# Decoder layer on one core: the weighed values of cross attention turned and divided by VectorE in 32x32 blocks, in place of transposes on TensorE and bank copies

## What is computed

```
q, k, v = x @ Wq, x @ Wk, x @ Wv             # q and k are then rotated
w   = softmax(q k^T / 4 + mask)              # over the tokens of x
a_w = tanh(gate) * softmax(q a_k^T / 4)      # over the adapter, a_k = ctx @ Wk
attn = w @ v + a_w @ a_v                     # per head
x = layernorm(x + attn @ Wo)
```

## Time and profile before

| | us |
|---|---|
| median of three runs | 2985.49 (2984.8 to 2992.0) |
| the profiled execution | 2984.0 |
| its span, first to last instruction | 2982.2 |
| batch 3 of the cross attention (units 48 to 63) | 127.93 |
| TensorE, VectorE, ScalarE busy in it | 121.03, 87.25, 87.03 |

### The profile page before, as it was taken

How to read it: one execution, slowest core, us unless ns; L and a number is a source line. 1 busy time by engine, 2 the same in 40 slices (tenths; PEclk the granted TensorE clock), 3 DMA queues, 4 the chain that set the end, 5 groups by cost and what they waited for, 6 DMA issues and landing times. The chain is left out here.

```text
span 2982.2 us, 81906 instructions
## 1 busy us (share of the span) xinstructions
PE 2804.6 (94%) x34646; PEld 1760.8 (59%) x34646; DVE 1748.8 (59%) x4940; ACT 1383.8 (46%) x3313; POOL 503.1 (17%) x626
## 2 busy tenths in 40 slices
PE   7999999999999999999998789999999999976999
PEld 3555555555656565656565566666666666654466
DVE  5565556555555555555565256666767666676533
ACT  3443434343434343434342166666766666664131
POOL 1212121212212121212121210101111010200020
PEclk9999999999999999999998799999999999998999
DMA  5010101101101111011011000000000000000451
GB/s 187 14 45 20 35 21 31 33 13 30 44 7 38 31 30 34 13 30 36 10 30 58 19 12 12 1 12 1 12 12 1 12 1 12 1 2 9 153 212 64
DMA packets 96922, 100.10 MB, mean 34 GB/s; under 512 B 38192, under 2 KB 84528, under 8 KB 95408
## 3 DMA queue, kind: packets, MB, share of 16 engines
q1 hardware_dynamic: 96400, 94.35, 9.9%
q0 software_dynamic: 160, 0.52, 0.0%
HBM read 90.01 MB, written 4.85 MB: 32 GB/s over the span
## 5 line engine op out<-in xcount | busy, mean ns | idle before, releaser
L209 PE MATMUL dr_p<-x_t,dr_w_g 128*128 128x512 f32 x1536 | 740.0, 608 | 11.0 <-DMA dr_w_g<-in_w_in 7.6
L1283 ACT ACTIVATE xa_probs<-xa_probs,xa_low 128x256 f32<-128x256 f32 x1024 | 436.4, 497 | 47.6 <-DVE xa_low L1414 45.7
L209 PEld LDWEIGHTS dr_p<-x_t,dr_w_g 128*128 128x128 f32 x1536 | 268.0, 191 | 226.4 <-issue 216.2
L1414 DVE CUSTOM_DVE_ANT_0 xa_probs<-xa_s,xa_mask 128x256 f32<-128x256 f32 x512 | 214.2, 418 | 261.5 <-PE xa_s L1194 261.3
L1207 PEld LDWEIGHTS xa_t<-ident,xa_probs 128*128 128x128 f32 x2048 | 222.5, 142 | 131.1 <-issue 77.6
L645 DVE SCALAR_TENSOR_TENSOR dr_acc<-dr_p,dr_taps,dr_acc 128x510 f32<-128x510 f32 (+2 forms) x384 | 285.1, 743 | 23.4 <-ACT dr_acc L501 15.5
L1207 PE MATMUL xa_t<-ident,xa_probs 128*128 128x128 f32 x2048 | 286.1, 280 | 7.7 <-DVE xa_probs_t L1423 5.9
L1289 ACT ACTIVATE xa_probs_t<-xa_t 128x512 f32<-128x512 f32 x256 | 152.8, 597 | 248.0 <-PE xa_t L1207 246.4
L1414 DVE CUSTOM_DVE_ANT_0 xa_probs<-xa_s,xa_zeros 128x256 f32<-128x256 f32 x512 | 214.7, 419 | 0.0
L1423 DVE COPY xa_probs_t<-xa_t 128x512 f32<-128x512 f32 x256 | 176.4, 689 | 42.1 <-PE xa_t L1207 28.1
L1222 PE MATMUL xa_o<-xa_probs_t,xa_val 128*32 128x128 f32 x4096 | 140.1, 278 | 44.9 <-DVE xa_probs_t L1423 24.8
(11 more groups left out here) (314 smaller groups left out, 4897.2 us busy)
## 6 DMA issues: line engine op xcount, KB each, us to landing
dr_alpha<-alpha_rows SPq DMA_DIRECT2D x64, 254.0 KB, 4.2
dr_w_g<-in_w_in SPq DMA_DIRECT2D x48, 256.0 KB, 6.0
dr_alpha<-alpha_rows SPq DMA_DIRECT2D x32, 256.0 KB, 5.4
ff_wide<-in_fw_qkv SPq DMA_DIRECT2D x8, 1024.0 KB, 14.2
x_t<-in_x_t SPq DMA_DIRECT2D x4, 1024.0 KB, 7.1
tokens<-in_x_tok SPq DMA_DIRECT2D x1, 4096.0 KB, 15.6
dr_wo_g<-in_w_out SPq DMA_DIRECT2D x8, 512.0 KB, 3.7
xa_ctx_b<-in_ctx_t SPq DMA_DIRECT2D x8, 512.0 KB, 3.9
```

The source lines that it names most:

```text
L209: mm = pe.matmul(bank[:, :], w_g[:, k, m, :], x_t[:, k, 2 * S * batch:2 * S * (batch + 1)], start=(k == 0), stop=(k == KC - 1))
L1283: op = act.activation(at, at, ACT.Exp, bias=low[:, v % 3, i, kind:kind + 1], scale=-1.0)
L1414: op = dve.tensor_tensor_reduce(out=probs[:, v % 3, i, kind, :], in0=bank_s[i][:, kind * S:(kind + 1) * S], in1=mask[:, par, q, :] if kind ...
```

## The change

VectorE now does the whole of `norm` itself, by a function `norm(v, g)` that runs after its first copy at every even unit (from unit 2 on) and once more after the loop. It turns `bank_o` in 32x32 blocks straight into `mixed` (the blocks stay where they are, each one is turned in itself), which brings the tokens of a block onto its partitions and the columns and sums of a head side by side along the free side. The same reciprocals, products and addition follow, in SBUF, into `joined`; a second block transpose turns the result back into `attn_t`, which has two halves now. The pieces `norm` and `turn` go from `early`, from TensorE and from the use of `bank_p`; ScalarE's copies L1313 and L1270 go. `out` waits for the four blocks of its tile. The gate is laid out by partition on the host, as 128x8 in place of 128x32.

```diff
         def early(u):
             b, d = divmod(u, HALVES)
-            if d % 2 == 0:
-                return ("norm", u // 2 - 1) if u else None
-            if d == 9:
-                return "turn", QT * b
-            if d == 1:
-                return ("turn", QT * b - 1) if b else None
             if d == 15:
...
-            elif what == "norm":
-                wait(pe, mixed_taken, at + 1)
-                for n in range(4):
-                    mm = pe.transpose(bank[:, n * P:(n + 1) * P], mixed[:, n * P:(n + 1) * P], ident)
-            elif what == "turn":
-                wait(pe, normed, XT * (at + 1))
-                for k in range(KC):
-                    mm = pe.transpose(bank[:, k * P:(k + 1) * P], attn[:, at % 2, k * P:(k + 1) * P], ident)
...
-                wait_taken(pe, ("turn", at))
+                wait(pe, normed, XT * (at + 1))
                 for k in range(KC):
-                    mm = pe.matmul(bank[:, :], attn_t[:, k, :], w_o[:, k, :], start=(k == 0), stop=(k == KC - 1))
+                    mm = pe.matmul(bank[:, :], attn_t[:, at % 2, k, :], w_o[:, k, :], start=(k == 0), stop=(k == KC - 1))
...
-                if u % 2:
-                    g = u // 2
-                    wait(act, weighed, 8 * (g + 1))
-                    if g:
-                        wait(act, made, made_at["norm", g - 1])
-                    act.activation(mixed[:, :], bank_o[:, :], ACT.Copy).then_inc(mixed_taken, 1)
...
+        def norm(v, g):
+
+            t, tile = g % XT, g // XT
+            blocks = mixed[:].rearrange("p (k h q x d) -> p k h q x d", k=2, h=2, q=4, x=2)
+            wait(v, weighed, 8 * (g + 1))
+            v.transpose(mixed[:, :], bank_o[:, :]).then_inc(mixed_taken, 1)
...
+            wait(v, mixed_taken, g + 1)
+            for h in range(2):
+                op = v.reciprocal(shares[:, :, h], blocks[:, :, h, :, 1 - h, 0])
...
+            v.tensor_tensor(joined[:].rearrange("p q h d -> p h q d"), parts[:, 0], parts[:, 1], ALU.add).then_inc(norm_step, 1)
+            if t == 0 and tile >= 2:
+                wait(v, made, made_at["out", tile - 2])
+            wait(v, norm_step, 4 * g + 4)
+            v.transpose(attn_t[:, tile % 2, t, :], joined[:].rearrange("p q h d -> p (q h d)")).then_inc(normed, 1)
...
                 copy(u, 0)
+                if u and u % 2 == 0:
+                    norm(dve, u // 2 - 1)
                 if early(u):
```

More of the change, by code:

```diff
@@ L1000, in cross_phase @@
         a = Space(nc, stack, "xa_")
-        gains = a.sb("gains", [P, XT, 2, 4])
+        gains = a.sb("gains", [P, XT, 2])
         zeros = a.sb("zeros", [P, S])
@@ L1090, in outer @@
             return late(u) if early(u) else None
-        TAIL = [("norm", LAST // 2 - 1), ("turn", QT * B - 1), ("out", QT * B - 1), ("count", B - 2), ("spread", B - 1),
+        TAIL = [("out", QT * B - 1), ("count", B - 2), ("spread", B - 1),
                 ("count", B - 1)]
@@ L1097, in cross_phase @@
         order += TAIL
-        BY_DVE = ("qt0", "qt1", "kt0", "kt1", "norm", "out", "count")
+        BY_DVE = ("qt0", "qt1", "kt0", "kt1", "out", "count")
         made_at, taken_at, bank_of, previous = {}, {}, {}, {}
@@ L1265, in act_take @@
                                     bank[:].rearrange("p (a h d) -> p a h d", a=PAIRS, h=2), ACT.Copy)
-            elif what == "spread":
+            else:
                 wait(act, ranked, NC * at)
                 op = act.activation(score_rows[:, :], bank[:, 0:S], ACT.Copy)
-            else:
-                op = act.activation(attn_t[:], bank[:].rearrange("p (k n) -> p k n", k=KC), ACT.Copy)
             op.then_inc(taken_act, 1)
@@ L1290, in copy @@
                     .then_inc(copied[0], 1)
-            act.activation(gains[:].rearrange("p t h i -> p t i h"), gate_in[:].rearrange("p (t i h) -> p t i h", t=XT, i=4),
-                           ACT.Tanh).then_inc(gains_made, 1)
+            act.activation(gains[:].rearrange("p t h -> p (t h)"), gate_in[:, :], ACT.Tanh).then_inc(gains_made, 1)
             for use in order[:len(PROJECT)]:
@@ L1329, in dve_take @@
                                 sin[:, None, :].to_broadcast([P, 2, S]), ALU.mult).then_inc(taken_dve, 1)
-            elif what == "norm":
-                t, slot = at % XT, at // XT % 2
-                blocks = bank[:].rearrange("p (k h i x d) -> p k h i x d", k=2, h=2, i=4, x=2)
-                if at == 0:
-                    wait(v, gains_made, 1)
-                wait(v, made, made_at[use])
-                for h in range(2):
-                    op = v.reciprocal(shares[:, :, h], blocks[:, :, h, :, 1 - h, 0])
-                op.then_inc(norm_step, 1)
-                wait(v, norm_step, 2 * at + 1)
-                v.tensor_tensor(shares[:, 1], shares[:, 1], gains[:, t], ALU.mult).then_inc(norm_step, 1)
-                wait(v, norm_step, 2 * at + 2)
-                for h in range(2):
-                    op = v.tensor_tensor(parts[:, :, h], blocks[:, :, h, :, h, :],
-                                         shares[:, :, h, :, None].to_broadcast([P, 2, 4, XD]), ALU.mult)
-                op.then_inc(taken_dve, 1)
-                wait_taken(v, use)
-                if t == 0 and at >= 2 * XT:
-                    wait(v, made, made_at["turn", at // XT - 2])
-                v.tensor_tensor(attn[:, slot, t * P:(t + 1) * P].rearrange("p (i h d) -> p h i d", i=4, h=2),
-                                parts[:, 0], parts[:, 1], ALU.add).then_inc(normed, 1)
             elif what == "count":
@@ L1365, in dve_take @@
                 v.bn_aggr(moments[:, at // QT, at % QT, :], stats[:, at, :]).then_inc(averaged, 1)
+        def norm(v, g):
[3 more added lines that the diff above has]
+            v.transpose(mixed[:, :], bank_o[:, :]).then_inc(mixed_taken, 1)
+            if g == 0:
+                wait(v, gains_made, 1)
+            wait(v, mixed_taken, g + 1)
+            for h in range(2):
+                op = v.reciprocal(shares[:, :, h], blocks[:, :, h, :, 1 - h, 0])
+            op.then_inc(norm_step, 1)
+            wait(v, norm_step, 4 * g + 1)
+            v.tensor_tensor(shares[:, 1], shares[:, 1], gains[:, t, :, None].to_broadcast([P, 2, 4]), ALU.mult).then_inc(norm_step, 1)
+            wait(v, norm_step, 4 * g + 2)
+            for h in range(2):
+                op = v.tensor_tensor(parts[:, :, h], blocks[:, :, h, :, h, :],
+                                     shares[:, :, h, :, None].to_broadcast([P, 2, 4, XD]), ALU.mult)
+            op.then_inc(norm_step, 1)
+            wait(v, norm_step, 4 * g + 3)
+            v.tensor_tensor(joined[:].rearrange("p q h d -> p h q d"), parts[:, 0], parts[:, 1], ALU.add).then_inc(norm_step, 1)
[3 more added lines that the diff above has]
+            v.transpose(attn_t[:, tile % 2, t, :], joined[:].rearrange("p q h d -> p (q h d)")).then_inc(normed, 1)
         def rate(v, b):
@@ L1445, in dve_all @@
             choose(dve, B - 2)
+            norm(dve, LAST // 2 - 1)
             for use in TAIL:
@@ L1989, in host_cross @@
         mask=f(i["mask_Bx1xSxS_fk0"].reshape(8, 2, 128, 256).transpose(0, 2, 1, 3)),
-        x_gate=f(np.broadcast_to(i["L0_xattn_gate"].reshape(1, 32), (128, 32))))
+        x_gate=f(np.repeat(i["L0_xattn_gate"].reshape(4, 4, 2).transpose(1, 0, 2).reshape(4, 8), 32, axis=0)))
 def cross_constants():
```

6 lines of the change are left out of this document (3 added, 3 removed).

## The result

The changed kernel takes 3027.57 us (median of four runs, 3026.7 to 3029.9), the kernel before beside it 2988.74: ratio 1.013, 95% interval 1.0118 to 1.0142. The profiled execution took 3029.86 us, its span is 3028.1, 45.9 us more than the 2982.2 of before. TensorE is busy for 14.7 us less (2789.9 against 2804.6) and the kernel is slower all the same.

The account below looks back on a forecast made before the run. TensorE's waits for VectorE's copy ahead of `weigh`, no longer covered by projections, were to bound it. From 2984.0 us, +20.7 without the clock and +10.4 for clock falls gave 3015.1; the median forecast was 3016, range 2998 to 3028.

Parts of the forecast that it names:

- The wait ahead of `weigh`: Units without an outer piece: TensorE waits about 0.87 us for VectorE's copy, which no projection hides.
- the 0.25 us in the next unit's scores: Unit behind one without an outer piece: VectorE reads the last scores late, so score matmuls take 1.39 us, not 1.14.
- rival (e): The 0.25 us doesn't add up in rows of such units; only the last batch loses: 2990 us, chance 0.08.
- (d): TensorE's work counts, copies are hidden, transposes and their idle time go: 72 us less, 2913 us, chance 0.05.
- The block transposes: VectorE's division at even places: 0.71 us out of a bank, 0.3 in SBUF; 1.08 more in all with waits.
- the cover: Units with a projection: 0.65 us of slack on VectorE, so its longer division costs nothing there.
- Rival (c): Block transpose out of a bank costs double a copy, 1.4 us; units without cover pay 9 us: 3026, chance 0.10.
- the read of ak0: Place 7: ScalarE reads ak0 from `bank_p` late, behind table load and exponentials; TensorE waits 1.3 us, unit takes 10.04.
- rival (b): ScalarE doesn't hold up place 7, its read starting earlier: seven times 1.3 us less, 3007 us, chance 0.10.
- The clock: Longer TensorE idle at place 0 and in the last batch: eight new clock falls at 1.3 us, 10.4 us.
- Rival (a): No new clock falls, all else as forecast: 3006 us, chance 0.22.
- the term behind the loop: After the loop the last division goes straight to `out` without two trips to TensorE and ScalarE: -1.0 us.

Follow-up runs that it names:

- run 1: Changed kernel with projections without an early piece put behind turn_probs again, ahead of `weigh`, except x0, x1 and qt0: 2990.51 us, ratio 0.9995.
- run 4: Changed kernel with the 512-column block transpose made twice into the same tile in each division: 3044.3 us, ratio 1.0175.
- Run 2: Changed kernel with ScalarE's `root` moved from place 5 to 6 and VectorE's `rate` from 6 to 7: 3026.52 us, ratio 1.0122.
- run 7: Changed kernel with projections behind turn_probs again, `choose` at the end of place 3, `count` at 5, `rate` at 9, `root` at 8: 2983.99 us, ratio 0.9984.
- run 5: Changed kernel with 16 added 128x128 transposes on TensorE ahead of x0 at place 0, overwritten by x0: 3021.34 us, ratio 1.011.
- run 6: Changed kernel with 2 added 128x512 matmuls on TensorE ahead of x0 at place 0, overwritten by x0: 3024.57 us, ratio 1.0116.
- run 12: The changed kernel once more, without any edit: 3028.58 us against 2991.05 for the kernel before, one run each.
- Run 8: Kernel before with only `choose`, `count`, `rate` and `root` moved, `norm` and `turn` left on TensorE: 2984.0 us, ratio 0.9987.
- run 9: Changed kernel with the table of gates kept 32 columns wide as before, its first 8 used: 3023.57 us, ratio 1.0109.

## Why the prediction was right

**Unit by unit, the mechanism held.** Before, forecast and measured (batch 3; places 2 to 15):

| place | before | forecast | after |
|---|---|---|---|
| 2 | 8.89 | 8.63 | 8.58 |
| 3 | 8.06 | 8.31 | 8.36 |
| 6 | 10.12 | 8.63 | 8.58 |
| 7 | 8.48 | 10.04 | 10.08 |
| 8 | 8.52 | 8.40 | 8.34 |
| 9 | 8.06 | 8.63 | 8.67 |
| 15 | 5.55 | 5.85 | 5.88 |

The sum over places 2 to 15 was +1.33 in the forecast and is +1.2 in the trace. The wait ahead of `weigh` (0.83 to 0.88), the 0.25 us in the next unit's scores, and that it comes in every such unit, are all in the rows; rival (e) falls with them, and (d) with run 1. Two readings of the waits were off. The prediction counted waits for VectorE's copy alone and expected about 100; it is 50, and the other 50 are for ScalarE's, which ends at nearly the same time. And the 31 waits of the earlier trace rows are not just those of units without an outer piece: six are of 0.44 us at place 1, behind the short piece x1, and place 0, which has x0 as its outer piece, waited 1.0 us in the row that the prediction didn't read. Neither enters its sum, which goes by the lengths of units.

**TensorE's busy time** was to fall by nearly 49 us and fell by 14.7. The transposes did go, but the same matmuls take longer where they wait for banks or run at the low clock: in total 183.2 us for the scores against 162.2, 146.1 for `weigh` against 140.1. The prediction had put the 0.25 us a unit into the lengths and left it out of this sign.

**VectorE.** The block transposes were put at 0.71 and 0.3 us; groups of the changed kernel, idle ahead last:

```profile
L1328 DVE STREAM_TRANSPOSE xa_mixed<-xa_o 128x512 f32<-128x512 f32 x64 | 45.1, 705 | 0.0
...
L1347 DVE STREAM_TRANSPOSE xa_attn_t<-xa_joined 128x128 f32<-128x128 f32 x64 | 19.9, 311 | 3.2
```

The division takes 2.34 us (forecast 2.35), the cover is 0.64 (forecast 0.65). Rival (c) is out, and run 4 shows that it would have cost more than the 9 us that I gave it, 17.0: I had counted the 0.7 us for 13 units, and not that more units of the last batch would fall.

**ScalarE.** Place 6 gained 1.54 and place 7 lost 1.60, by the read of ak0 that the prediction named (6.3 us in six waits; rival (b) counted seven, but batch 0 has no root and the last batch no ak0). Rival (b) is out. Run 2 adds that the table load is a cost that wanders: it delays the first copy or the read that follows it, wherever the root is put (0.87 to 1.32 us of wait in runs 1, 2 and 7).

**The clock.** Falls were forecast at six places 0, one in batch 0, and one more in the last batch, 8 x 1.3 = 10.4 us. The trace has five new ones, at places 0 and 1 of batches 2 to 6, none in batch 1 and one in batch 0. The sixth place 0 that was counted, that of the last batch, had fallen in the kernel before already (8.55 us, and 7.38 at its place 1), so it was no new one. The mis-sized term is the price of one at place 0: the five batches are on average 4.18 us longer than before, the forecast without clock says 2.4, so 1.8 a batch; batch 3, where runs of like kind can be set side by side (run 5), 2.4. The low clock reaches on into place 1, where `weigh` and the next scores are slow too. Fewer falls at a higher price make about 11 us in all.

By the rule that the prediction cites from the Trainium skill, TensorE: Matmul & The Clock Gate, Part 4 (transposes don't count toward the full clock as other matmuls do), run 5 should have kept the falls and run 6 lost them. Run 5 has one in its batches 2 to 6 and run 6 two: the measurement decides against the rule in this case.

Rival (a), no falls, is out too.

**Units in sum:** 20.7 + 1.0 (the term behind the loop left out) + 10.4 = 32.1 forecast; 32.7 in the first trace of the changed kernel and 37.1 in the second (run 12). The 4.3 us between them are falls, 5.0 more in the last batch and 0.7 less in batch 0, so the agreement to half a microsecond is luck, and the one fall more that I counted there is a matter of the execution.

**The tail** was forecast as -1.0; from the start of unit 126 to the end of `out` it is 23.48 us against 21.38, +2.1. TensorE behind unit 127, in the changed kernel and in the one before:

```profile
2776.55 5.94 PE L1169 MATMUL xa_p<-x_t,xa_attn_t 128*128 128x512 f32 x8 [3.78 <-DVE xa_attn_t L1347]
```

```profile
2733.17 0.63 PE L1168 MATMUL xa_p<-ident,xa_mixed 128*128 128x128 f32 x4 [0.86 <-ACT xa_mixed L1313]
2735.31 0.63 PE L1172 MATMUL xa_p<-ident,xa_attn 128*128 128x128 f32 x4 [1.51 <-DVE xa_attn L1349]
2736.72 3.67 PE L1183 MATMUL xa_p<-x_t,xa_attn_t 128*128 128x512 f32 x8 [0.78 <-ACT xa_attn_t L1270]
```

From the end of the last `weigh` to `out` it is 3.78 us now and was 4.4, a gain of 0.6. What turns it is the clock: it fell in the wait of 3.78 us, and `out` takes 5.94 in place of 3.67. But the comparison rests on one execution of the kernel before. Run 8 has its three short waits (0.86, 1.51, 0.78), nothing of the change, and the fall all the same:

```profile
2729.01 6.17 PE L1183 MATMUL xa_p<-x_t,xa_attn_t 128*128 128x512 f32 x8 [0.78 <-ACT xa_attn_t L1270]
```

Against it (24.31 us from the start of unit 126 to the end of `out`) the changed kernel is 0.8 ahead, close to the forecast. The clock fell ahead of `out` in all twelve traces with the edit and in one of the two without, so the sign of this term isn't settled. The other 3.8 us behind the loop lie in the feed-forward part, whose first stretch runs at a lower clock in this execution (mean of the 10 us from 50 us behind the start of unit 126: 0.69, before 1.00 in the same stretch). Run 8, which has nothing of the change, spends 267.0 us there too, run 5, which has all of it, 264.5; so I don't put this down to the change.

**What stays open.** The forecast was 3016 and the median is 3027.57. Of these 11.6 us, 3.3 are the base: the forecast stood on 2985.5, the median of before is now 2988.74. The other 8 are the last batch's falls, up to 5 in one execution and none in another, and what lies outside the units. That is 13.2 us between the two profiled executions, but 44.6 - 37.1 = 7.5 with the second trace of the changed kernel, and the profiled execution of before was near the low end of its runs (2984.0 of 2983.2 to 2995.6). Part of it is the delta attention, which the prediction put at nothing since the edit doesn't touch its code: 2.9 to 6.0 us by 1654 us, in all twelve traces with the edit and in neither of the two without. The stalls at L272 that belong to it have no releaser in the trace, and they aren't a matter of the addresses that run 9 put back. The other theory of run 9, that it comes with the shorter program, fits its result, but no run changes that alone, so the cause stays open. That the whole came out within 0.4% is in part luck: for the clock, one place too many and a price too low cancel to within a microsecond.

## What to carry to other kernels

Ask of a piece that is to be removed what it stands in front of. Here the transposes and the projection hid a copy of 0.7 us; once they were gone or moved, TensorE waited ahead of `weigh` in 102 of 128 units, mostly for 0.85 us, where it had waited in 45, and a busy total that fell by 15 us told nothing of it. Then the longer chain on the other engine has to be given a cover in each place where it runs: a unit without one cost more than its wait in most batches, since the clock fell too, and a large piece of work moved there, with the other moves of run 7, made the same change win 1.0%.

## What the runs showed of the hardware

- A block transpose of 128x512 float32 out of a bank takes 0.705 us, one of 128x128 in SBUF 0.311 us; the copy of 128x512 out of a bank beside them takes 0.690.
- Fillers in idle time can keep the granted clock: with 1.7 us of transposes more at place 0, places 0 and 1 of batch 3 took 2.39 us less together (clock 1.00 in place of 0.85 and 0.73), though the transposes stand on the engine that was to be relieved.
- The same instructions with the same waits can keep or lose the clock. A wait of 2.93 us at place 0 was followed by `weigh` in 1.08 us in batch 1 and in about 1.94 in batches 3 to 6. Behind the loop of the kernel before, waits of 0.86, 1.51 and 0.78 us were followed by `out` in 3.67 us in one trace and, in run 8, in 6.17.
- The delta attention has the same code in all kernels. By 1654 us it is 2.9 to 6.0 us behind the trace of the kernel before in all twelve traces that hold the edit (3.2 and 5.6 in two executions of one and the same kernel), and 0.8 ahead in the other trace without it.
